# First attention of a two-layer decoder: every fourth head's second relation term added by TensorE with a diagonal matrix, and one copy of that head moved to VectorE

## What is computed

```python
attn_scores = jnp.einsum('bihd,bjhd->bhij', q, k) / scale
li = x @ rel_W[:, :d].T
lj = x @ rel_W[:, d:].T
logits = li[:, :, None, :] + lj[:, None, :, :] + rel_b
relation_probs = jax.nn.softmax(logits, axis=-1)
bias = jnp.einsum('bijk,hk->bhij', relation_probs, logical_bias)
gate = jax.nn.sigmoid(x @ gate_W.T + gate_b)
gate = jnp.transpose(gate, (0, 2, 1))[..., None]
attn_scores = attn_scores + gate * bias
attn_weights = jax.nn.softmax(attn_scores, axis=-1)
out = jnp.einsum('bhij,bjhd->bihd', attn_weights, v).reshape(b, s, d)
```

## Time and profile before

| | |
|---|---|
| median of 3 runs | 6172.91 us (6155.47 to 6177.64) |
| the profiled execution | 6178.81 us |
| its span, first to last instruction | 6177.0 us |
| mean granted clock of TensorE | 0.948 of 2.4 GHz |
| first attention, first to last `u` and transposes | 171.7 to 1558 us of the span |
| busy in the whole span: PE, DVE, ACT, POOL | 87%, 64%, 51%, 38% |

### The profile page before, as it was taken

The page is one execution under the profiler, slowest core; times in us unless marked ns, Lnnn a source line. Parts: engine busy times, 40 slices in busy tenths (PEclk is TensorE's granted clock), DMA queues, the critical chain, the costliest instruction groups (busy, mean ns, idle before and its releaser), DMA issues. The chain is left out here.

```text
span 6177.0 us, 139507 instructions
## 1 busy us (share of the span) xinstructions
PE 5370.6 (87%) x53888; PEld 3328.1 (54%) x53888; DVE 3941.3 (64%) x6854; ACT 3130.6 (51%) x4743; POOL 2346.6 (38%) x1998
## 2 busy tenths in 40 slices
PE   7788888888897798798888899978899997999998
PEld 3455555555685444577777788854233332444444
DVE  5899999999787555444444344456888884333333
ACT  5899999999456554222222233243366665111111
POOL 1787877788565333344444321144200000000000
PEclk9899999999998999799999999988899998999999
DMA  5102020200111243333233311045423222000000
GB/s 169 41 23 44 13 53 13 47 14 12 56 41 63 90 153 152 109 109 102 99 105 106 105 47 57 33 101 145 110 44 48 47 44 74 14 20 15 19 20 12
DMA packets 416040, 396.15 MB, mean 64 GB/s; under 512 B 231650, under 2 KB 370136, under 8 KB 407248
## 3 DMA queue, kind: packets, MB, share of 16 engines
q1 hardware_dynamic: 401616, 362.68, 21.2%
q10 hardware_dynamic: 13824, 25.17, 1.1%
HBM read 247.50 MB, written 140.23 MB: 63 GB/s over the span
## 5 line engine op out<-in xcount | busy, mean ns | idle before, releaser
L538 POOL TENSOR_SCALAR attn_u<-attn_rel,attn_aux 128x1024 f32<-128x1024 f32 x512 | 1091.0, 2131 | 272.2 <-DVE attn_nm L565 272.1
L689 PE MATMUL attn_tp<-attn_ident,attn_pr 128*128 128x128 f32 x4096 | 576.5, 285 | 238.6 <-ACT attn_pt L628 236.5
L3318 DVE TENSOR_REDUCE attn_mx<-attn_mp 128x1 f32<-128x512 f32 x1024 | 652.6, 685 | 91.6 <-PE attn_mp L3397 90.6
L689 PEld LDWEIGHTS attn_tp<-attn_ident,attn_pr 128*128 128x128 f32 x4096 | 453.0, 144 | 459.7 <-ACT attn_pt L628 320.1
L557 DVE SCALAR_TENSOR_TENSOR attn_u<-attn_rel,attn_aux,attn_u 128x1024 f32<-128x1024 f32 x512 | 681.6, 1331 | 28.0 <-POOL attn_u L538 19.6
L649 ACT ACTIVATE attn_pr<-attn_pr,attn_nm 128x1024 f32<-128x1024 f32 x512 | 605.9, 1183 | 89.0 <-DVE attn_nm L565 88.8
L3382 ACT ACTIVATE attn_pt<-attn_st 128x1024 f32<-128x1024 f32 x512 | 506.7, 1023 | 283.0 <-PE attn_st L3408 282.4
L565 DVE CUSTOM_DVE_ANT_0 attn_pr<-attn_u,attn_s 128x1024 f32<-128x1024 f32 x512 | 618.7, 1209 | 48.1 <-PE attn_s L680 32.8
L628 ACT ACTIVATE attn_pt<-attn_tp 128x512 f32<-128x512 f32 x1024 | 570.0, 628 | 11.3 <-PE attn_tp L689 11.1
L3774 PE MATMUL moe_ps<-moe_w,moe_hidt 128*128 128x512 f32 x1024 | 453.2, 593 | 0.0
L3397 PE MATMUL attn_mp<-attn_kt,attn_qt 96*128 96x512 bf16 x1024 | 371.7, 393 | 17.5 <-DMA attn_qt<-s_q 16.5
(11 more groups left out here) (492 smaller groups left out, 10223.4 us busy)
## 6 DMA issues: line engine op xcount, KB each, us to landing
s_qkv<-gin_qkv SPq DMA_DIRECT2D x32, 1536.0 KB, 5.1
core_qk<-s_qkv SPq DMA_DIRECT2D x32, 1024.0 KB, 5.1
attn_qt<-s_q SPq DMA_DIRECT2D x384, 64.0 KB, 2.9
attn_kt<-s_k SPq DMA_DIRECT2D x192, 128.0 KB, 4.4
core_arow<-s_alr SPq DMA_DIRECT2D x32, 512.0 KB, 3.7
core_grow<-s_gar SPq DMA_DIRECT2D x32, 512.0 KB, 3.7
core_vv<-s_qkv SPq DMA_DIRECT2D x32, 512.0 KB, 3.6
s_o<-core_o ACTq DMA_DIRECT2D x32, 512.0 KB, 2.8
```

What stands on the lines that cost most here:

```text
L538: pool.tensor_scalar(u[:, x % 4], rel[:, z % 2, 1], aux[:, s, 4 + NH + h:5 + NH + h], aux[:, s, 4 + 2 * NH + h:5 + 2 * NH + h], ALU.mult, ...
L689: ins = pe.transpose(tp[k][:, n], pr[:, x % BUF, (4 * k + n) * P:(4 * k + n + 1) * P], ident[:])
L3318: dve.reduce_max(mx[w % 2][:].rearrange("p h t a -> p (h t a)")[:, j:j + 1], bank(("row", number))[:], AX.X).then_inc(m["max_done"], 1)
```

## The change

Heads 3, 7, 11 and 15 of each tile are treated in another way (`onto(x)`).

- VectorE makes no mix for them. Its score takes `u` as GpSimd left it, and waits for `u_done`.
- ScalarE makes a diagonal matrix of these heads' weights: the identity, 128 by 128, times the head's `w0` by rows, in f32, four heads ahead, in one of two buffers `dg`.
- TensorE adds `diag(w0) @ rel[0]` to the head's scores in PSUM: two f32 products of 128 rows and 512 columns after the two bf16 ones.
- The second of these heads' two copies out of PSUM moves from ScalarE to VectorE (`second_copy`), where it stands three positions on: after mix y+3, before score y+2. `pt_done` becomes two semaphores, one for each half.

```diff
+        dg = r.sb("dg", [P, 2, P])
...
+        onto = lambda x: x % GR == GR - 1
+        rel_out = lambda z: rel[:, z % 2, 0]
...
             def score(v, x):
 
-                dve.wait_ge(m["mix_done"], head(v, x) + 1)
+                if onto(x):
+                    dve.wait_ge(m["u_done"], head(v, x) + 1)
+                else:
+                    dve.wait_ge(m["mix_done"], v * (STREAM - STREAM // GR) + x - x // GR + 1)
...
+            def second_copy(v, y):
+                dve.wait_ge(m["tp_done"], head(v, y) * 2 + 2 + 2 * BUF)
+                if begun(v, y - 2 * GR):
+                    dve.wait_ge(m["pv_done"], v * (STREAM // GR) + y // GR + 1)
+                dve.tensor_copy(pt[:, y % (2 * GR), 4:8], tp[1][:]).then_inc(m["pt_done1"], 1)
...
                 for x in range(STREAM):
-                    mix(v, k, x)
+                    if not onto(x):
+                        mix(v, k, x)
+                    if onto(x - 3) and begun(v, x - 3):
+                        second_copy(v, x - 3)
                     if begun(v, x - 1):
                         score(v, x - 1)
             score(BODIES - 1, STREAM - 1)
+            second_copy(BODIES - 1, STREAM - 1)
...
-                for k in range(2):
+                for k in range(1 if onto(y) else 2):
                     act.wait_ge(m["tp_done"], head(v, y) * 2 + k + 1 + 2 * BUF)
-                    act.activation(pt[:, y % (2 * GR), 4 * k:4 * k + 4], tp[k][:], ACT.Copy).then_inc(m["pt_done"], 1)
+                    act.activation(pt[:, y % (2 * GR), 4 * k:4 * k + 4], tp[k][:], ACT.Copy).then_inc(m[f"pt_done{k}"], 1)
+
+            def diagonal(v, k, x):
+
+                z, h = x // NH, x % NH
+                if begun(v, x - 2 * GR):
+                    act.wait_ge(m["qk_done"], head(v, x) - 2 * GR + 1)
+                at = aux[:, slot_of(k, z), 4 + h:5 + h]
+                act.activation(dg[:, x // GR % 2], ident[:], ACT.Copy, scale=at).then_inc(m["dg_done"], 1)
...
+                    if onto(x) and not (final(v, z) and h == NH - 1):
+                        diagonal(v, k, x + GR)
...
-                    ins = pe.matmul(sc[x % 2][:, n], qt[:, z % 2, h], kt[:, h, n * 512:(n + 1) * 512], start=True, stop=True)
+                    ins = pe.matmul(sc[x % 2][:, n], qt[:, z % 2, h], kt[:, h, n * 512:(n + 1) * 512], start=True, stop=not onto(x))
+                if onto(x):
+                    pe.wait_ge(m["rel_done"], tile(v, z) + 1)
+                    pe.wait_ge(m["dg_done"], v * (STREAM // GR) + x // GR + 1)
+                    for n in range(2):
+                        ins = pe.matmul(sc[x % 2][:, n], dg[:, x // GR % 2], rel_out(z)[:, n * 512:(n + 1) * 512], start=False, stop=True)
                 ins.then_inc(m["qk_done"], 1)
...
-                        pe.wait_ge(m["pt_done"], head(v, x) * 2 + k - 1)
+                        pe.wait_ge(m[f"pt_done{k}"], head(v, x))
```

More of the change, by code:

```diff
@@ L429, in stage_attn0 @@
                  "ex_done sum_done ln_done rel_done "
-                 "u_done mix_done ns_done qk_done exp_done tp_done pt_done pv_done os_done ot_done row_done out0 out1 chain")
+                 "u_done mix_done ns_done qk_done exp_done tp_done pt_done0 pt_done1 dg_done pv_done os_done ot_done row_done out0 out1 chain")
         m = {n: r.sem(n) for n in names.split()}
@@ L642, in _ @@
             relation_end(0, 0)
+            act.wait_ge(m["id_in"], 16)
+            diagonal(0, 0, GR - 1)
             for v, k, b in bodies(act):
@@ L695, in weigh @@
                 if piece == 0:
-                    pe.wait_ge(m["pt_done"], head(v, GR * (g + 1)) * 2)
+                    for half in range(2):
+                        pe.wait_ge(m[f"pt_done{half}"], head(v, GR * (g + 1)))
                     if g % GR == 0:
```

## The result

The changed kernel takes **6217.4 us** (median of 4, 6214.4 to 6229.2) against 6174.7 before (4 runs): a ratio of 1.0079, with a 95% interval of 1.0055 to 1.0104. That is slower by 0.8%, about 43 us. The forecast was no change (6175 us); the time lies in the range of 6118 to 6235, but the change made the kernel slower by more than the interval. The first attention's last TensorE work starts at 1611.6 us of the span instead of 1560.6. These 51 us are more than the 40.5 by which the two spans differ (6217.5 and 6177.0), so all of the loss is in that stage. The 10 us that came back lie in the last stage, which the change does not touch: the same 512 products of 128x512 on TensorE (L3750, L3784 after) took 274.8 us in the profiled execution before and 261.0 in this one, at a mean granted clock of 0.95 and 0.97 in the last 670 us.

A forecast was written before the change was run, and what follows sets the result against it. VectorE and ScalarE were taken to share the bound of the first attention's tile. Stretch A's +0.7 and stretch B's −0.65 sum to +0.05 us per tile, 2 us over 32 tiles: 6175 us, no change, range 6118 to 6235.

The forecast's parts named there:

- A: Exponential 0 to score product 13, 31.7 us: ScalarE works without a gap, VectorE has little slack; forecast +0.7 us per tile.
- B: Product 13 to exponential 0, 10.8 us: VectorE is the late engine; forecast −0.65 us per tile.
- Two engines share the bound: First attention's mean tile, 43.4 us: VectorE busy 41.2 and ScalarE 40.7, TensorE with some 8 us to spare.
- TensorE's pair: Two f32 products in each changed head hold TensorE's queue 0.9 us, 3.6 per tile, taken up almost wholly by its waits.
- the copy's waits: VectorE's copies wait for transposes: 0.32 us at head 3, 0.58 at head 7, over 1 at head 11.
- Transposes 7 keep their place: Head 7's transposes on TensorE don't move, ScalarE's lighter copies and added diagonals nearly cancelling; they end at 21.55 us.
- this rival: Four passes: the f32 pair costs twice as much, scores 3 and 7 start later; +1.4 us per tile, 6218 us; chance 0.06.
- the walk: Stretch A followed in order from score 0's end: mixes −2.40, copies +1.83, clashes +0.37, waits +1.29, so +1.1 us.
- ScalarE's own gain doesn't count, as it then waits for VectorE: Stretch A: three half copies −1.44 and two diagonals +0.56 us on ScalarE are left out of the sum.
- The diagonals' price: Each of four 128-column diagonals per tile takes 0.28 us in ScalarE's queue, bounds 0.2 to 0.45.
- TensorE's pair reaches the copy: The pair pushes the transposes, VectorE's copy waits 0.9 us longer at heads 7 and 11; +1.8 per tile, 6231; chance 0.19.
- The faster rival: Transposes 3 and 7 end before VectorE asks, no waits form; −1.5 us per tile, 6124 us; chance 0.33.

The follow-up runs named there:

- e1: The changed kernel with half of the f32 pair, the diagonal's product for keys 512 to 1023 left out: 6201.1 us, ratio 1.0053.
- e2: The changed kernel with the diagonal's product left out whole, diagonals still made and the copy still on VectorE: 6203.7 us, ratio 1.0054.
- e3: The changed kernel with both copies of every head on ScalarE again, f32 product kept: 6193.1 us, ratio 1.0036.
- e4: The changed kernel with one diagonal made at the start and used for all heads: 6206.4 us, ratio 1.0059.
- e6: The changed kernel with no diagonal product and both copies on ScalarE, diagonals still made: 6130.0 us, ratio 0.9928.
- e7: The kernel before with the mixes of heads 3, 7, 11 and 15 left out and nothing put in their place: 6101.2 us, ratio 0.9883.
- e9: The changed kernel with only the product's operands in bf16, the copy staying on VectorE at its place: 6206.0 us, ratio 1.0062.
- e11: The changed kernel with the product in bf16, both copies on ScalarE and the diagonals made by GpSimd: 6101.7 us, ratio 0.9890.
- e10: The changed kernel with the product in bf16 and both copies on ScalarE, diagonals still on ScalarE: 6138.4 us, ratio 0.9952.

## Where the prediction was right and where it was wrong

**The stretches.** The prediction cut the tile at exponential 0 and product 13. The same cut in the other kernels (us, medians of clean tiles; before and changed are the tiles shown):

| kernel | A: exponential 0 to product 13 | B: product 13 to exponential 0 |
|---|---|---|
| before | 31.7 | 10.8 |
| forecast | 32.4 | 10.15 |
| changed | 33.7 | 10.9 |
| e1, half of the pair | 33.1 | 10.7 |
| e2, no pair | 33.1 | 10.8 |
| e3, copy on ScalarE | 32.8 | 11.0 |
| e4, one diagonal | 33.4 | 10.7 |
| e6, no pair, copy on ScalarE | 32.3 | 9.5 |
| e7, and no diagonals | 31.7 | 9.3 |

The forecast lacks 1.3 us in A and 0.8 in B.

**The bound, right.** "Two engines share the bound" and the loop of two stretches hold: with nothing put in their place, four mixes (4.8 us) are worth 1.6 us a tile (e7), all of it in B, and A keeps its 31.7.

**TensorE's pair, wrong.** This is the first step that failed: "such a product takes 0.593 alone and 453.2/1024 = 0.44 in a row ... so a pair holds the queue 0.9 us". I divided by the profile's instructions and took them for calls. The pair takes 1.72 us. The trace of before had the means to see it. Its products with the values are 8 calls a head in f32, 4096 in all, and the row counts twice that:

```profile
L704 PE MATMUL attn_op<-attn_pt,attn_v x8192: 272/273/423, 192.5 to 1559.6; 128*32 128x128 f32 x200
```

while the bf16 score product has as many instructions as calls, 1024:

```profile
L680 PE MATMUL attn_s<-attn_kt,attn_qt x1024: 377/382/634, 155.2 to 1550.6; 96*128 96x512 bf16 x171
```

The page of the Trainium skill that I set against the rows ("FP8 and Floating Point Precision", TensorE Precision Notes: four passes) agrees with the trace after all. Two bf16 products take 0.61 us and one 0.38, so they start some 0.23 apart; four times that is 0.92 for a call, and an f32 call takes 0.86 (1.72 for the pair). My sign against the forecast, f32 products 0.85 us apart, came true, and so did the tile time outside 42.5 to 44.5. I gave this rival 0.06 and a time of 6218. That the time came out so is in part luck: the rival counted +1.4 us a tile for the pair's second half, and half a pair less (e1) gives back 0.8; e2 and e9, without its cost, are still at 6204 and 6206.

**The place of the transposes and the copy's waits, right in kind and too small.** The second step that failed is "Transposes 7 keep their place", and the same taken for transposes 3. They end 10.9 and 21.6 us after exponential 0 in the kernel before, and 11.6 and 22.6 in the changed one; in e1, with the pair as I had priced it, transposes 7 end at 22.2. Copy 7, score 9, the relation sum and the logarithm stand behind that. In e1 score 3 waits 0.84 us where I had walked 0.39, and the copies of heads 3 and 7 wait 0.27 and 0.95 where I had 0.32 and 0.58; without the pair in the way (e2) they wait 1.14 and 0.95, and in the changed kernel, where the waits at products 3 and 7 come first, 0 and 0.24. At head 11 the copy waits 2.33 us in e1 and in the changed kernel. That isn't to be held against the 0.58 of the walk, which comes on top of the 1.16 us that score 13 had waited for product 13 before; I had said over 1. But score 13 starts 2.5 us behind product 13, where the walk had 2.16.

ScalarE's diagonals are part of this. The diagonal of head 7 stands ahead of the copies that transposes 3 wait for, and the walk let it cancel against lighter copies and then counted nothing. With one diagonal for all heads (e4) both stretches are 0.3 us shorter, and with neither pair nor copy on VectorE the diagonals lengthen A by 0.6 (e7 to e6). The forecast summed A and B to +0.05 us a tile; e1 has +1.3, and the pair's second half adds 0.8. So the larger error is here, and not in the pair: with the pair as priced I was 1.25 us a tile short. How that divides between the copy's waits and the diagonals, no run separates.

**"ScalarE's own gain doesn't count, as it then waits for VectorE", right.** It lost 1.9 us of copies, and its waits for scores rose from 59.0 to 96.8 us.

**The diagonals' price, right** (0.30 for 0.28), but they are worth 11 us in the changed kernel, where the walk had them at nothing.

**The rivals.** "TensorE's pair reaches the copy" named +0.9 us at heads 7 and 11, and its 6231 was 14 us too high. The copy of head 11 waits the same 2.33 us with half the pair, so the rest of the pair was not felt there; it was felt at scores 3 and 7 (1.70 and 0.70 us). The faster rival fell: the waits formed in every kernel with the copy at its place. What I had not written down as a rival is what e6 shows, that pair and copy hide each other, so that undoing either one gives back little.

**The clock.** Fewer tiles are lengthened after the change (6 of 31 instead of 11), and the mean granted clock went from 0.948 to 0.953. Between 67 us by the clean tiles and the 51 of the stage lie the 16 us that this, and a few shorter tiles at the stage's end, are worth, an effect that I had named for the faster rival alone. That the filling of TensorE's pauses did this fits e2, where the pauses are back and the stretch has 0.95; it was not tried by itself.

## What to carry to other kernels

Check how many instructions a call makes (the count of a row against the loops of the code) before dividing a row's time by its count. A small step that waits for another engine, put into the queue of an engine whose results a third one needs at once, costs its wait each time. Moving it behind the urgent step is no sure cure: here it cost 27 us with one product and gave 44 with another, so it has to be measured in the kernel as it will stand. And when one of two late steps is removed without effect, take away both before calling either harmless: here 14 and 24 us alone were 87 together, and the idea of the change, in bf16, with the copy left alone and the diagonals on GpSimd, was worth 1.1%.

## What was unexpected of the hardware

An f32 product of 512 columns is two instructions of 592 ns, and the four of a pair take 1.72 us in the queue, 0.43 each, so a call takes 0.86 us; f32 transposes are one instruction each (4096 for 4096 calls). In bf16 the same product is one instruction of 379 ns (e11). A 128 by 128 diagonal written in bf16 takes GpSimd 0.37 us in the median (e11), where ScalarE takes 0.47 (e10) and, written in f32, 0.39.
